# A fused attention and spiking feed-forward layer on one core: broadcasts of the softmax sums first among the small products, block transposition ahead of the cosine product, sum transposes behind the weighting

## What is computed

```python
h = layernorm(xn) * ln_scale + ln_bias
q, k, v = (h @ w_down_q.T) @ w_up_q.T, (c := h @ w_down_kv.T) @ w_up_k.T, c @ w_up_v.T   # 16 heads of 64
scores = rope(q) @ rope(k).T / 8
out = softmax(scores) @ v @ w_out.T + xn
y = relu(xn @ W_fc.T) ** 2 @ W_proj.T          # 512 hidden features
ffn = (spikes of a 5-step integrate-and-fire neuron fed with y) / 5
```

## Time and profile before

| | |
|---|---|
| median of three runs | 1110.21 us |
| profiled execution | 1110.22 us, span 1108.4 us |
| TensorE clock granted | 0.995 of full |
| TensorE busy | 1050.3 us, 95% |
| ScalarE busy | 930.4 us, 84% |
| VectorE busy | 908.6 us, 82% |
| GpSimd busy | 894.9 us, 81% |
| DMA | 217.96 MB, mean 197 GB/s |

### The profile page before, as it was taken

How to read it: one execution, slowest core, us unless ns; L and a number is a source line. 1 busy time by engine, 2 the same in 40 slices (tenths; PEclk the granted TensorE clock), 3 DMA queues, 4 the chain that set the end, 5 groups by cost and what they waited for, 6 DMA issues and landing times.

```text
span 1108.4 us, 26191 instructions
## 1 busy us (share of the span) xinstructions
PE 1050.3 (95%) x6880; PEld 711.4 (64%) x6880; DVE 908.6 (82%) x1223; ACT 930.4 (84%) x3136; POOL 894.9 (81%) x897
## 2 busy tenths in 40 slices
PE   3789999999999999999999999999999999999987
PEld 3556666666666666666666666666666666666654
DVE  3788888888888888888888888888888888888872
ACT  3789888888888888988888888888888888898871
POOL 3677888888888888888888888888888898888861
PEclk9899999999999999999999999999999999999999
DMA  5287768777777877777877777877777787777773
GB/s 181 89 216 210 200 187 218 205 204 196 200 201 200 218 201 196 203 202 195 229 197 192 212 195 194 221 203 204 199 199 202 200 218 201 196 200 202 189 199 92
DMA packets 93281, 217.96 MB, mean 197 GB/s; under 512 B 22464, under 2 KB 43200, under 8 KB 93120
## 3 DMA queue, kind: packets, MB, share of 16 engines
q1 hardware_dynamic: 92864, 216.52, 73.6%
q10 hardware_dynamic: 384, 1.05, 0.4%
HBM read 7.77 MB, written 4.19 MB: 11 GB/s over the span
## 4 chain that ended last, share of the span: by engine, by line
PE 48%; DVE 15%; ACT 14%; issue 13%; SPq 6%; DMA 2%; DVEq 1%; ACTq 1%; POOL 0%; POOLq 0%
PE ps_s L328 12%; PE ps_u L342 12%; PE ps_b L447 10%; ACT prob L538 7%; DVE neg_max L688 6%; SPq L254 5%; PE ps_a L383 5%; PE ps_qk L318 4%; PE ps_qk L319 2%; DVE turned L699 2%; DVE latent L727 2%; DVE qk L683 2%; DMA gathered<-turned 2%; ACT raw L550 2%; ACT spread L562 2%
## 5 line engine op out<-in xcount | busy, mean ns | idle before, releaser
L538 ACT ACTIVATE prob<-ps_s,neg_max 128x256 f32<-128x256 f32 x1024 | 473.8, 484 | 93.8 <-DVE neg_max L688 93.0
L833 POOL TENSOR_TENSOR partner<-partner,rope_sb 128x512 f32<-128x512 f32 x256 | 326.7, 1276 | 137.1 <-DMA partner<-raw 134.6
L688 DVE TENSOR_REDUCE neg_max<-ps_s 128x4 f32<-128x1024 f32 x256 | 309.9, 1211 | 101.8 <-PE ps_s L328 100.7
L836 POOL TENSOR_TENSOR qk<-qk,partner 128x512 f32<-128x512 f32 x256 | 326.3, 1275 | 20.1
L699 DVE STREAM_TRANSPOSE turned<-prob 128x1024 f32<-128x1024 f32 x256 | 315.3, 1232 | 1.2 <-ACT prob L538 0.2
L328 PE MATMUL ps_s<-qk 64*128 64x256 f32 x2048 | 292.7, 405 | 3.4 <-ACT prob L538 2.4
L342 PE MATMUL ps_u<-gathered,ckv 128*64 128x256 f32 x2048 | 277.5, 392 | 7.0 <-DMA gathered<-turned 5.5
L328 PEld LDWEIGHTS ps_s<-qk 64*128 64x128 f32 x2048 | 177.8, 187 | 112.3 <-issue 92.1
L538 ACT ACTIVATION_READ_ACCUMULATOR prob<-ps_s,neg_max 128x1 f32 x1024 | 220.2, 215 | 0.0
L683 DVE TENSOR_TENSOR qk<-ps_qk,rope_sb 128x512 f32<-128x512 f32 x256 | 175.0, 684 | 41.7 <-ACT raw L550 34.9
L550 ACT COPY raw<-ps_qk 128x512 f32<-128x512 f32 x256 | 155.2, 606 | 48.9 <-PE ps_qk L319 48.5
(11 more groups left out here) (67 smaller groups left out, 909.2 us busy)
## 6 DMA issues: line engine op xcount, KB each, us to landing
gathered<-turned SPq DMA_DIRECT2D x1016, 128.0 KB, 2.4
partner<-raw SPq DMA_DIRECT2D x256, 256.0 KB, 2.4
x_sb<-in_x SPq DMA_DIRECT2D x32, 128.0 KB, 2.2
resid<-early SPq DMA_DIRECT2D x32, 128.0 KB, 2.0
out<-out_sb SPq DMA_DIRECT2D x32, 128.0 KB, 2.0
turned<-in_wup SPq DMA_DIRECT2D x2, 512.0 KB, 5.7
gathered<-turned ACTq DMA_DIRECT2D x8, 128.0 KB, 4.4
rope_sb<-in_rope SPq DMA_DIRECT2D x1, 512.0 KB, 6.8
```

Source lines behind the costliest of these rows:

```text
L538: last = nc.scalar.activation(prob[:, s % 2, :, h, :, t, :].rearrange("p j k c -> p k j c"), ps_s[:, s % 2, h, t, :].rearrange("p (k j c) ...
L688: nc.vector.tensor_reduce(neg_max[:, s % 2, :, :], ps_s[:, s % 2, :, :, :], AXIS_X, ALU.max, negate=True).then_inc(max_ready, 1)
L833: nc.gpsimd.tensor_tensor(other, other, sin_sb, ALU.mult).then_inc(sin_ready, 1)
L836: nc.gpsimd.tensor_tensor(qk[:, s % 4, :, :], qk[:, s % 4, :, :], other, ALU.add).then_inc(rope_done, 1)
```

## The change

Four things are moved; nothing is added or removed, and no size changes.

- TensorE, `extras`: the broadcast of the sums comes ahead of the feed-forward product in p2 and p3 (in p0 it stays behind the latents, in p1 it is alone).
- TensorE, p7: the transposes of the output sum and of the reciprocals go from ahead of `weigh_latents` to behind it.
- ScalarE: in p0, `copy_u` and the first `copy_spread` go ahead of the copies of the latents, right behind the exponentials; in p1 to p3, `copy_spread` goes ahead of the exponentials, right behind the copy of the projection.
- VectorE: in every step, `turn` comes ahead of `rotate`, and so also ahead of `split_latents` in p1 and the moments in p2.

```diff
@@ TensorE, extras
+                if p < 4 and not outside(b - 1, LAST):
+                    broadcast_rden(b - 1, p)
                 if not outside(b, B) and p in (2, 3):
                     ffn_out(b, p - 2)
                 if not outside(b + 1, B) and p in (5, 6):
                     ffn_in(b + 1, p - 5, 1 - b0)
-                if p < 4 and not outside(b - 1, LAST):
-                    broadcast_rden(b - 1, p)
                 if p == 7:
                     if not outside(b + 3, B):
                         transpose_inputs(b + 3, 1 - b0)
-                    if not outside(b - 1, B):
-                        transpose_sum(b - 1)
-                    if not outside(b, LAST):
-                        transpose_rden(b)
@@ TensorE, step
                 if not outside(g, STEPS):
                     weigh_latents(g, s, i)
+                if p == 7 and not outside(b - 1, B):
+                    transpose_sum(b - 1)
+                if p == 7 and not outside(b, LAST):
+                    transpose_rden(b)
@@ ScalarE, step
                     copy_projected(g + LEAD["project"], s + LEAD["project"], i)
+                if p in (1, 2, 3) and not outside(b - 1, LAST):
+                    copy_spread(b - 1, p)
...
                     exponentials(g + LEAD["scores"], s + LEAD["scores"], i)
+                if p == 0 and not outside(g, STEPS):
+                    copy_u(g, s, i)
+                if p == 0 and not outside(b - 1, LAST):
+                    copy_spread(b - 1, 0)
                 if p == 0:
...
-                if p < 4 and not outside(b - 1, LAST):
-                    copy_spread(b - 1, p)
-                if not outside(g, STEPS):
+                if p > 0 and not outside(g, STEPS):
                     copy_u(g, s, i)
@@ VectorE, step
+                if not outside(g + LEAD["turn"], STEPS):
+                    turn(g + LEAD["turn"], s + LEAD["turn"], i)
                 if not outside(g + LEAD["project"], STEPS):
                     rotate(g + LEAD["project"], s + LEAD["project"])
...
-                if not outside(g + LEAD["turn"], STEPS):
-                    turn(g + LEAD["turn"], s + LEAD["turn"], i)
```

## The result

| | before | change |
|---|---|---|
| median of the runs, us | 1110.43 (1109.39 to 1112.67, 4 runs) | 1084.75 (1083.63 to 1085.78, 4 runs) |
| profiled execution: its time, its span, us | 1110.22, 1108.4 | 1083.63, 1081.8 |
| mean granted TensorE clock | 0.995 | 0.993 |

The ratio of the times is 0.9765, with a 95% interval from 0.9749 to 0.9781: 25.7 us faster. The forecast of 1088.4 us lies 3.7 us above, and the range holds the result.

A forecast was written before the change was run, and what follows sets the result against it. TensorE, 95% busy, was taken as the bound, with an SP and DMA chain ending 0.2 us before p4's weighting. Gains of 11.9 + 9.9 = 21.8 us from 1110.22 gave 1088.4 us, range 1077 to 1101.

The forecast's parts named there:

- The transposes of p7: In p7, the weighting goes ahead and covers TensorE's wait for VectorE's sum: 29 x 0.41 = 11.9 us gained.
- ScalarE in p0 and the wait of p1: The first `spread` copy ends earlier, so TensorE's broadcast wait in p1 goes: 0.55 us in first batches, 0.34 in second.
- The broadcasts and copies in p1 to p3: The fourth `spread` copy comes before p4's output product, whose 0.24 us wait goes; p3's exponentials neither lose nor gain.
- VectorE and the cosine product: The cosine product ends each step, so TensorE's projections wait 0.1 us in p2 and p3: 0.2 us a batch lost.
- The chain of DMAs: SP's transfers feeding p4's weighting come only 0.38 us earlier, capping the gain up to there: 26 x 0.38 = 9.9 us.
- the first rival: TensorE alone sets the end and gains all its waits, 20.0 us plus 11.9 in p7: 1078.3 us; chance 0.17.
- The page on issuing engines: Counter-evidence for p4: issue is small beside transfer, twelve transfers take an estimated 3.6 us, so DMAs would not limit.
- The sum: Whole kernel: 11.9 us from p7 plus 9.9 from 26 loop batches, 21.8 us off 1110.22, giving 1088.4 us; chance 0.50.

## Why the prediction was right, and where it was not

- **The transposes of p7: right, too large.** 11.9 us were forecast for 29 batches. Undone they cost 8.7, alone they gave 8.8. The term took the wait's full 0.41 us and left out the 0.09 for the other weight shape: 29 x 0.32 = 9.3. Nothing behind `finish` came late, as said: the next maxima start 1.27 us after the first scores both before and after.
- **ScalarE in p0 and the wait of p1: right in place, low in size.** The wait cost 0.65 us, not 0.55. Besides 0.55 us in front of the broadcast there were 0.10 between it and the weighting: 526.15 - 525.72 = 0.43 before, 511.17 - 510.84 = 0.33 after.
- **The broadcasts and copies in p1 to p3: right in effect, but not needed for it.** "The fourth copy is then there some 1.7 us before the output product of p4, so that product's 0.24 us go too" holds: with VectorE's order undone the product still follows at once. But VectorE's order does the same by itself, which the prediction didn't see, so p4 loses nothing where both the copies and the broadcasts are put back. What this part does bring is 5.2 us in p2, where the broadcast covers a wait that the prediction didn't have. In p4 the wait was worth 0.33 us, not 0.24.
- **VectorE and the cosine product: a step that failed.** In p2 0.14 us were measured for the cosine product (0.1 forecast), in p3 none (0.1 forecast). That the 0.14 is so near is partly luck: the product ends 7.99 us after the first scores and not 8.20, since I added lengths as shown, where VectorE starts the next operation up to 0.1 us before the shown end, and TensorE wants it at 7.91 and not at 8.07. I overlooked what stands behind it in VectorE's queue. The sentence "VectorE takes their remainder in p1 behind two other operations, so it doesn't wait for them" is true, but TensorE's `ffn_out` waits for the remainder: 0.25 us more in p2.
- **The chain of DMAs: there, but it did not set the time.** The sentence "The smaller one counts: 0.38 in both" made the DMAs the limit of p4, with a wait in most batches. That step failed: the changed kernel has 5 such waits in all, and in the loop TensorE's own order sets the batch. The size was too small, since SP took 0.03 us and not 0.15 to follow `raw` (no row gave the 0.15), so in the first batch the DMAs came 0.52 us earlier instead of 0.38, and in the second 0.58. TensorE came 0.59 and 0.44 us earlier (weighting of p4 after first scores: 18.12 to 17.53, 17.89 to 17.45). In both batches the weighting found its blocks in place, with 0.2 and 0.3 us to spare. This is the first rival's mechanism, but with the cosine and latent waits, which keep it from that rival's 1078.3 us. That the chain is real and near is shown: undoing VectorE's order put the exchange back to 7.28 us and brought 28 waits for DMAs.
- **The page on issuing engines.** The Trainium skill, page DMA: Bandwidth & Descriptors, section "Issuing engines are not separate DMA queues", says that issue is usually small beside the transfer. The twelve issues take 7.54 us after the change too, and the run with VectorE's order undone has TensorE waiting for what they bring. So in this chain issue is the larger part, against 2.4 us from the last issue to its landing, and the measurement decides. An issue takes SP 0.57 us for the first of p0's four DMAs, when the DMA engines are a third busy (0.33 from 509.20 to 511.00), and 0.59 for the last of the twelve; each lands 2.3 to 2.4 us later. That fits a pace set by issuing. But the DMA engines are 93% busy while the twelve are issued (513.40 to 520.90), so no run excludes that they would soon set the same pace.
- **The sum.** In the loop's 24 batches 24 x (0.41 + 0.38) = 19.0 us were forecast and 19.9 came. That it is so near is luck in part: p7 was 0.09 a batch too high and the rest of the batch 0.13 too low, by another limit than the forecast's. At the end 0.7 us came against 1.2. The largest error is the start: 6.0 us came before batch 4, where the sum has 2 x 0.79 = 1.6. It put the batches before the loop at nothing, and 3.2 us came there. How much of this is the new order is open, since starts differ: the kernel with the longer written-out end has the same order up to there and reaches batch 4 at 187.26, 2.7 us after the change's 184.53.
- **How the parts add.** Undone one by one they cost 8.7 + 17.8 + 4.0 + 5.2 = 35.7 us, more than the 25.7 of all together. On the kernel before, p7 alone gives 8.8 and VectorE's order 12.3. The sum of these is 21.1, which leaves 4.6 for ScalarE's part and the broadcasts. VectorE's order is worth more with the rest around it (17.8) than alone (12.3), because without it what TensorE gains in p1 is lost again at the DMAs: in the 24 batches alone it is 10.3 us against 6.4. These sums hold the starts too, which differ by some us, so only their large differences count.

## What to carry to other kernels

Between two in-order engines a wait is often not removed but moved to the next place at which they meet, so for each wait that you take away, follow both queues to the next meeting: here 0.65 us gained in p1 gave 0.39 back in p2. Work that needs nothing belongs in front of work that waits, but check that "nothing" includes the return of its output buffer; with one product moved away from in front of the weighting, on top of two other edits, 24 us were lost. And find every chain that ends at the same instruction before summing gains: the DMA chain, with 0.2 us of slack, ate 10.3 us in 24 batches where VectorE's part, which moves it earlier, was undone.

## What the runs showed of the hardware

- An idle SP starts a DMA 0.03 us after the shown end of the copy that releases it (512.08 to 512.11, and 0.02 to 0.03 in the other p1 of the loop).
- SP takes 0.57 us to issue a DMA of 128 KB when the DMA engines are a third busy and 0.59 when they are 93% busy; both land 2.3 to 2.4 us after their issue starts.
- Twelve DMA issues of the same shape take 7.54 us in looped code, evenly, and 7.5 to 9.1 us, unevenly, in the same code written out; two issues of the exchange take 1.15 us looped, and 2.10 and 2.28 us in two of eight written-out batches. Transfers of instructions appear in the written-out stretch (32 packets from 700 to 960 us) and not in the loop's (none from 200 to 700 us). What slows the issues is not shown.
- Where TensorE goes from `128*128` to `128*64` weights, the next matmul starts about 0.09 us later than without the switch: 0.31 against 0.22 us behind a pair of transposes in p7, 0.96 against 0.87 behind four output products in p4 and p5.
